# Two layers of graph, attention and expert work on one core: routed experts placed inside the shared expert, and the first attention's keys-values product made narrower

## The reference, cut to what matters

```
# L0_mix, for each of 12 heads of 64, M = 256 random features
phi_q = relu(einsum('bhnd,md->bhnm', q, random_features)); phi_k = relu(...k...)
kv = einsum('bhnm,bhnd->bhmd', phi_k, v)
attn = einsum('bhnm,bhmd->bhnd', phi_q, kv) / M
# L1_ffn, xf = tokens x 768, 8 routed experts of hidden size 1536, top 2 of them for each token
g_s = silu(einsum('td,edf->etf', xf, Wg_s)); u_s = einsum('td,edf->etf', xf, Wu_s)
shared_out = einsum('etf,efd->td', g_s * u_s, Wd_s)
top_vals, top_idx = top_k(xf @ W_router + expert_bias, 2); rw = softmax(top_vals)
routed_out = sum over a token's two experts of rw * ((silu(xf @ Wg_r) * (xf @ Wu_r)) @ Wd_r)
x = x + shared_out + routed_out
```

## Time and profile before

| | |
|---|---|
| median of 3 runs | 2142.15 us (2137.17 to 2149.9) |
| profiled execution, its own time | 2149.02 us |
| its span, first to last instruction | 2147.3 us |
| mean granted PE clock | 0.961 of full |
| PE busy in the span | 2003.2 us, 93% |
| DVE, ACT, POOL busy | 1311.4, 964.7, 89.9 us |

### The profile page before, as it was taken

One profiled execution on the slowest core, in us unless ns is written; L12 is line 12 of the kernel. 1 busy time (PEld: TensorE's weight loads), 2 busy tenths in 40 slices (PEclk: granted clock), 3 DMA queues, 4 the chain that ended last, 5 costly groups with the idle time before them and its releaser, 6 DMA issues. The chain is left out here.

```text
span 2147.3 us, 33807 instructions
## 1 busy us (share of the span) xinstructions
PE 2003.2 (93%) x13496; PEld 1890.5 (88%) x13496; DVE 1311.4 (61%) x1884; ACT 964.7 (45%) x1191; POOL 89.9 (4%) x70
## 2 busy tenths in 40 slices
PE   5899889999999999998999798999889999999996
PEld 4899779999999999997899698899878888888885
DVE  8455477444344345446466547552288988988986
ACT  6344422222111122124566433412167777777775
POOL 0000000000000000000010000000001001001001
PEclk9999789999999999998999889899989999999998
DMA  3311026111112031102200050332199999999997
GB/s 84 104 30 30 21 72 164 61 53 52 52 52 69 31 89 50 44 26 68 59 16 30 7 171 23 125 104 89 46 383 382 387 375 362 380 374 361 380 375 261
DMA packets 186546, 313.62 MB, mean 146 GB/s; under 512 B 13036, under 2 KB 87276, under 8 KB 186018
## 3 DMA queue, kind: packets, MB, share of 16 engines
q1 hardware_dynamic: 181346, 295.31, 39.3%
q0 software_dynamic: 4816, 16.62, 3.4%
q10 hardware_dynamic: 272, 0.07, 0.0%
HBM read 293.48 MB, written 20.40 MB: 146 GB/s over the span
## 5 line engine op out<-in xcount | busy, mean ns | idle before, releaser
L183 PE MATMUL psum<-re_whi,xt_sb 128*128 128x512 f32 (+1 forms) x1680 | 506.8, 376 | 1.6 <-DVE xt_sb L3189 1.6
L183 PE MATMUL psum<-ring_hi,xt_sb 128*128 128x256 f32 (+3 forms) x1920 | 359.1, 285 | 11.9 <-DVE m_v L617 3.9
L183 PEld LDWEIGHTS psum<-re_whi,xt_sb 128*128 128x128 f32 x1680 | 312.5, 188 | 47.0 <-issue 2.0
L3173 DVE TENSOR_TENSOR re_wlo<-moe_raw,re_whi 128x1536 fp32r<-128x1536 f32 x173 | 303.5, 1756 | 35.2 <-ACT re_whi L3127 34.1
L183 PEld LDWEIGHTS psum<-ring_hi,xt_sb 128*128 128x128 f32 (+1 forms) x1920 | 303.6, 190 | 13.2 <-issue 5.3
L183 PE MATMUL psum<-re_wlo,xt_sb 128*128 128x512 f32 (+1 forms) x840 | 312.8, 372 | 0.0
L3127 ACT ACTIVATE re_whi<-moe_raw 128x1536 fp32r<-128x1536 f32 x174 | 258.6, 1489 | 90.8 <-PE psum L183 89.1
L183 PE MATMUL psum<-ring_lo,xt_sb 128*128 128x256 f32 (+3 forms) x960 | 272.7, 284 | 0.0
L183 PEld LDWEIGHTS psum<-ring_lo,xt_sb 128*128 128x128 f32 (+1 forms) x960 | 182.8, 190 | 0.0
L183 PEld LDWEIGHTS psum<-re_wlo,xt_sb 128*128 128x128 f32 x840 | 158.5, 189 | 21.8
L3173 DVE TENSOR_TENSOR re_wlo<-re_more,re_whi 128x1536 fp32r<-128x1536 f32 x84 | 147.6, 1757 | 29.4 <-ACT re_whi L3127 29.4
(11 more groups left out here) (430 smaller groups left out, 3245.1 us busy)
## 6 DMA issues: line engine op xcount, KB each, us to landing
moe_raw<-in_L_ffn_Wg_r SPq DMA_DIRECT2D x74, 768.0 KB, 8.8
moe_raw<-in_L_ffn_Wu_r SPq DMA_DIRECT2D x58, 768.0 KB, 8.5
moe_raw<-in_L_ffn_Wd_r SPq DMA_DIRECT2D x42, 768.0 KB, 6.1
re_more<-in_L_ffn_Wd_r SPq DMA_DIRECT2D x42, 768.0 KB, 9.3
re_more<-in_L_ffn_Wu_r SPq DMA_DIRECT2D x30, 768.0 KB, 7.9
ring_raw<-in_L_gnn_w_rel SPq DMA_DIRECT2D x18, 896.0 KB, 5.1
re_more<-in_L_ffn_Wg_r SPq DMA_DIRECT2D x15, 768.0 KB, 7.2
ring_raw<-in_L_mix_W_qkv SPq DMA_DIRECT2D x24, 384.0 KB, 4.3
```

The costliest lines, as they stand in the source:

```text
L183: mm = pe.matmul(out, lhs[a], rhs[b], start=(first and i == 0), stop=(last and i == 2))
L3173: dve.tensor_tensor(wlo[:, i % RING, :], raw[i % RAWS], whi[:, i % RING, :].bitcast(F32), ALU.subtract)\
```

## The change

1. In the first attention (not the second) `kv` becomes one plane: a head's 64 columns hold the high part, and the other head's 64 columns, zero before, the low part. `attend` issues 16 matmuls in two groups, head 1 into `k.pair[1]`, head 0 into `k.pair[0]`. The two halves of each output are added: ACT copies one half into `at_f` (64 partitions, L612 of after), DVE adds the other. This replaces one ACT copy of 128 partitions.
2. The splits of the next pair's queries move from the end of a pair into the next pair's key tiles 1 and 2, and the split of the second head's keys behind query tile 0. `qk_hi` counts heads now, in both attentions, so `qk_low` starts after the first head's ACT copy.
3. The shared expert's second half moves behind the routed experts, into a block of its own (`phase_shared_last`). The routed block stands after the first half.
4. Job 0's rows are gathered, turned and split inside the first half's `down`, and so is its weight chunk 0 (`preset_low`). The loops start from counts given by small instructions (`credit`).
5. The last job is written out behind the loop and leaves out the work for a next job. In its place SP loads chunks 0 to 2 of the shared expert's second half, and ACT and DVE split chunk 0.
6. The last scatter stands at the start of `phase_shared_last`. `x` is then loaded back from `acc_dram`, the 10 output tiles are added to it, and six transfers store it, each after its tile.

```
             def attend(p):
-                groups = [(num_pair(hd), (2 * hd, 2 * hd + 1)) for hd in (1, 0)] if second else [(k.pair[0], range(4))]
...
+                for hd in (1, 0):
+                    for m in (2 * hd, 2 * hd + 1):
...
+                        for b in range(2):
+                            for h in range(2):
+                                mm = pe.matmul(num_pair(hd)[:, h, 0:HN], kv[:, 0, m, :], phiq[:, m, b, h * HN:(h + 1) * HN],
+                                               start=(m == 2 * hd and b == 0), stop=(m == 2 * hd + 1 and b == 1))
...
         def _(act):
+                    if not second and p >= 1 and t in (1, 2):
+                        qk_high(p, QUERIES, (t - 1,))
...
-                    act.wait_ge(s["at_mm"], p + 1)
-                    act.activation(halves(at_f[:, p, :]), k.pair[0][:, :, 0:HN], ACT.Copy).then_inc(s["at_out"], 1)
+                    for n, hd in enumerate((1, 0)):
+                        act.wait_ge(s["at_mm"], 2 * p + n + 1)
+                        act.activation(halves(at_f[own(hd), p, :]), num_pair(hd)[other(hd), :, 0:HN], ACT.Copy)\
+                            .then_inc(s["at_out"], 1)
...
         def _(dve):
+                for n, hd in enumerate((1, 0) if not second else ()):
+                    at_part = halves(at_f[own(hd), p, :])
+                    dve.wait_ge(s["at_out"], 2 * p + n + 1)
+                    dve.tensor_tensor(at_part, num_pair(hd)[own(hd), :, 0:HN], at_part, ALU.add).then_inc(s["num_f"], 1)
...
+            down(0)
+            turn_first()
+            down(1)
...
-            pe.wait_ge(s["gathered"], 16)
-            turn_gathered(0)
-            turn_gathered(1)
-            count = count_of(pe)
-            with pe.Fori(0, count) as j:
+            pe.sem_inc(s["x_mm"], 2)
+            last = last_of(pe)
+            with pe.Fori(0, last) as j:
+                job(j, False)
+            job(last, True)
...
-            sp.wait_ge(s["all_added"], 1)
-            for r in range(RAWS):
-                sp.wait_ge(loaded[r], count * (16 * NC // RAWS) + (SHARED_LOADS[r] + 16))
-                take_wait(sp)
-            sp.dma_start(out, k.acc_dram[0:NODES, :]).then_inc(s["stored"], 16)
+            src = shared_sources(*shared, 1)
+            for i, r in enumerate((1, 2, 4)):
+                wait_low(sp, last, RAWS + r)
+                take_wait(sp)
+                dst = k.moe_raw[:, i * WE_MOE:(i + 1) * WE_MOE].rearrange("p (k c) -> p k c", c=GC)
+                sp.dma_start(dst, src[i]).then_inc(k.last_loaded[i], 16)
...
+def phase_shared_last(k, name, wg, wu, wd, out):
...
+            load(RAW)
+            sp.wait_ge(s["last_added"], 16)
+            for t, r0, r1 in ROWS:
+                sp.dma_start(k.x[r0:r1, t, :], k.acc_dram[t * P + r0:t * P + r1, :]).then_inc(s["acc_in"], 16)
+            for i in range(RAW + 1, CH):
+                load(i)
+            for t, r0, r1 in ROWS:
+                sp.wait_ge(s["o_read"], TT + t + 1)
+                sp.dma_start(out[t * P + r0:t * P + r1, :], k.x[r0:r1, t, :]).then_inc(s["stored"], 16)
```

More of the change, by code:

```diff
@@ L317, in num_pair @@
         def num_pair(hd):
[L318 removed]
+            return k.pair[0] if hd == 0 else k.pair[3 if second else 1]
         @block.sync
@@ L568, in _ @@
                     act.activation(halves(phiq[:, m, 0, :]), src, FUNC).then_inc(s["pq_hi"], 1)
+                    if m == 0 and p + 1 < PAIRS and not second:
+                        qk_high(p + 1, KEYS, (1,))
                     if m == 0 and p + 1 < PAIRS and second:
@@ L579, in _ @@
                 act.wait_ge(s["kv_f"], p + 1)
-                act.activation(kv[:, 0, :, :], kvf[:], ACT.Copy).then_inc(s["kv_hi"], 1)
-                if p + 1 < PAIRS:
+                if second:
+                    ins = act.activation(kv[:, 0, :, :], kvf[:], ACT.Copy)
+                else:
+                    for hd in range(2):
+                        ms = slice(2 * hd, 2 * hd + 2)
+                        ins = act.activation(kv[:, 0, ms, own(hd)], kvf[:, ms, own(hd)], ACT.Copy)
+                ins.then_inc(s["kv_hi"], 1)
+                if p + 1 < PAIRS and second:
                     qk_high(p + 1, QUERIES)
@@ L696, in _ @@
                     ins.then_inc(s["pq_lo"], 1)
+                    if m == 0 and p + 1 < PAIRS and not second:
+                        qk_low(p + 1, KEYS, (1,))
                 if p >= 1 and p + 5 <= len(st.chunks):
@@ L2957 @@
+            for i in range(2 * TT):
+                c, t = divmod(i, TT)
+                x = k.x[0:TS[t], t, c * GC:(c + 1) * GC]
+                out_ready(dve, i)
+                dve.tensor_tensor(x, out_bank(i)[0:TS[t], 0:GC], x, ALU.add).then_inc(s["o_read"], 1)
+                if i in (TT, TT + 1):
+                    gathered_low(i - TT)
+                if i == TT + 2:
+                    preset_low()
 CH_COLS = 512
@@ L2994, in load_preset, with phase_routed_experts @@
     sp.dma_start(dst, src).then_inc(k.moe_loaded[LOADED_BY[i]], 16)
-def phase_routed_experts(k, name, routed, out):
+def phase_routed_experts(k, name, routed, shared):
     with ExitStack() as ctx:
@@ L3142, in gathered_high, with job @@
                                ACT.Copy).then_inc(s["x_hi"], 1)
-            act.activation(credit[:, 3:4], k.one[:], ACT.Copy).then_inc(s["silu"], HCH)
-            for i in range(HIGH_LEAD):
-                weight_high(0, i)
-            gathered_high(0, 0)
-            gathered_high(0, 1)
-            count = count_of(act)
-            with act.Fori(0, count) as j:
+            def job(j, is_last):
                 for i in range(NC):
@@ L3221, in _ @@
                         dve.tensor_copy(w_now[:], k.job_w[:, bass.ds(j, 1)]).then_inc(s["now_made"], 1)
-                    low(*next_chunk(j, i + LOW_LEAD))
+                    if i + LOW_LEAD < NC or not is_last:
+                        low(*next_chunk(j, i + LOW_LEAD))
+                if is_last:
+                    dve.wait_ge(s["next_hi"], 1)
+                    dve.tensor_tensor(next_lo, k.moe_raw[:, 0:WE_MOE], next_hi.bitcast(F32), ALU.subtract)
+            for n, (name_, by) in enumerate((("lo_done", RAWS + 1), ("used", RING), ("hf", HCH), ("x_lo", 2), ("from_made", 1))):
+                dve.memset(credit[:, 4 + n:5 + n], 0.0).then_inc(s[name_], by)
+            dve.memset(y, 0.0).then_inc(s["y_act"], 2)
+            dve.tensor_copy(to_now[:], k.job_to[:, JOBS:JC]).then_inc(s["now_made"], 1)
+            for i in range(1, LOW_LEAD):
+                low(0, i)
+            last = last_of(dve)
+            with dve.Fori(0, last) as j:
+                job(j, False)
+            job(last, True)
         @block.tensor
@@ L3306, in experts_block @@
         phase_router_shared(k, "rs", *shared, routed)
-        phase_routed_experts(k, "re", routed, out)
-SEM_SETS = (range(100, 160), range(160, 220))
-LASTING_SEMS = range(220, 232)
+        phase_routed_experts(k, "re", routed, shared)
+        phase_shared_last(k, "sl", *shared, out)
+SEM_SETS = (range(100, 158), range(158, 216))
+LASTING_SEMS = range(216, 232)
 class Kit:
```

558 lines of the change are left out of this document (351 added, 207 removed).

## The result

The changed kernel takes 2117.07 us (median of 4 runs, 2113.18 to 2122.08), the kernel before 2144.23 beside it (4 runs, 2137.17 to 2149.9). The ratio is 0.9874, 95% interval 0.9854 to 0.9895: 27 us faster, 3.4 less than the forecast of 30.6, and inside the range. The profiled execution of after has a span of 2111.4 us and is the fastest of its four; that of before was the slowest of its four.

The account below looks back on a forecast made before the run. PE was taken to bound the routed loop (40.17 us a job) and the first attention, with 31 us at the routed stage's ends not PE work. Terms sum to −30.6 us: 2142.15 becomes 2111.6, range 2100 to 2127.

Parts of the forecast that it names:

- what would show it wrong: PE waiting in jobs 0 to 2 for DVE's splits behind a late load, jobs over 40.2 us, or second shared half over 96.
- The start of the routed stage: Between shared half and job 0: PE's pause costs 2.4 instead of 13.8 us; with turning matmuls added, together −10.7 us.
- Chunk 0 is split already. Chunk 1 is not: Job 0's start: chunk 1 ready at 1555.5 at the earliest, PE done with chunk 0 at 1555.0; 0.5 us added.
- transfers too late: Rival, routed stage's start: PE starts job 0 12 us earlier, transfers don't; 3 to 6 us come back, 2117; chance 10%.
- a margin of 5 us: Job 0: chunk 9 lands near 1567, while PE wants it, less 3.4 us for splitting, near 1572.
- PE's clock behind the seam: Routed stage after its opening pause: 1.7 of the 2.7 us lost at lower clock remain, a gain of 1.0 us.
- Last job and new seam: Routed stage's end: last job drops six turning matmuls, −0.7 us; pause of 1.0 us before second shared half, +1.3 with slack.
- Tail: After PE's last matmul: 5.7 us, bounds 5.2 to 9.8, instead of 17.4, so −11.7 us.
- First attention: Eight fewer matmuls per pair −8.0, waits +1.7, shorter pause −1.0, DVE addition at the end +0.9: −6.4 us, bounds −9 to 0.
- The second rival, additions on the path: Rival, first attention: DVE not free in time in each pair, waits of 1 us and more take the saving; 2118; chance 15%.
- Second attention: DVE starts a split after ACT's first head, 0.7 us earlier, removing PE's waits in 5 pairs: −1.4 us, at worst 0.
- The slower rival: Routed loop: transfers set the pace; at 353 GB/s a job takes 42.3 us, at 345 the kernel takes 2155; chance 3%.

Follow-up runs that it names:

- with the read moved: Changed kernel with three-chunk splitting, early loads and stores, three loads issued ahead, plus PE reading the last job's number inside the shared block: 2105.55 us, 0.9808 of the kernel before.
- splits alone: Changed kernel, but ACT and DVE split chunks 0, 1 and 2 of job 0 inside the shared block, not only 0: 2116.68 us, 0.9865 of the kernel before.
- transfers alone: Changed kernel, but chunks 6 and 7 of job 0 and four stores of x are issued inside the shared block: 2111.99 us, 0.9837 of the kernel before.
- both with the loads ahead: Changed kernel with three-chunk splitting, early loads and stores, and loads of chunks 9 to 11 inside the shared block: 2104.68 us, 0.9809 of the kernel before.
- more stores: Changed kernel with another 1.9 MB of stores of x, to an unused tensor, before the first loop loads: 2128.3 us (one run).

## Why the prediction was right, point by point

The time came out as forecast because what it missed was of both signs, and that is luck. Between the two traces the routed stage is 10.0 us worse than forecast; the first attention is 8.5 better, the tail 2.0, the second attention 1.9, and 2.6 are not of the change. The prediction also named what would show it wrong: that PE waits in jobs 0 to 2 for DVE's splits behind a late load. PE did, in job 0. By its own sign the account of the routed stage's start was wrong.

**The start of the routed stage: size right, one consequence missed.** The pause is 2.16 us for 2.4. The read of the job number and the entry of the loop were given 1.0 us; with the read moved the pause is 1.52, so the read is worth 0.6 to 1.0 us at least, as DVE ends the pause there. The step that failed is the next one, "Chunk 0 is split already. Chunk 1 is not", with 0.5 us for it. It looked at the first wait only. The old 13.8 us of PE's pause were also the time in which ACT and DVE got their ring ahead: ACT had made six splits and DVE five when PE began. Now DVE owes eight, 13.4 us, before the first hidden product, which PE wants after 10.8.

**The rival "transfers too late" was the case, at 10%, and too cheap.** It was dismissed by a margin of 5 us: chunk 9 some 14 us behind PE's start at 384 GB/s, and wanted 19 us behind it. The margin was worked out wrong twice. Nine chunks of 2.1 us are the 19 us already, so with 3.4 for splitting off, the margin was some 2 us. And the chunk that PE waits through is not 9 but 12, whose split stands ahead of the second hidden product in DVE's program; PE wants that product after 81 matmuls, also some 19 us in. Chunk 9 came 17.5 us behind PE's start (1437.16 to 1454.67), 18.1 behind SP's first issue. Its issue stands at 1446.97, 4.5 us behind the end of the last store's issue, a step that was not counted. Its price was put at 3 to 6 us; the two pauses are 9.5 us and the clock behind them costs some 4, read from the same groups of products at full clock, so that the routed stage is 10 us over its forecast of 563.4 although the later jobs gave 2.1.

**PE's clock behind the seam** was taken as 1.7 us lost. With the pauses gone the stage takes 561.4 us, where 14 jobs of 40.01 less the 0.7 of the last one's turning are 559.4: 2.0 us lost, of which 1.6 are in the 45 products (12.11 for 10.49). The size was right where the clock fell, and it does not always fall: the 45 products took 12.11 to 12.14 us in five traces after pauses of 2.15 to 2.49 us, 10.83 and 10.49 in two after 2.16 and 2.17, and 10.49 in one after 1.52.

**Last job and new seam: right.** 0.93 us of pause for 1.0, and the clock stayed at full, as forecast (1.00 from 2010 to 2014 us). The half takes 96.3 us for 96.0, with a wait of 1.13 us for a split of DVE inside it that was there before too (1.15).

**Tail: right in kind, mis-sized.** 3.7 us for 5.7. The two issues take 0.67 together, not 0.6 each, and the landing with what follows it 2.4 for 3.9.

**First attention: the largest wrong size, −6.4 for some −10 to −15.** Eight matmuls less are 1.2 us a pair, as said. The pause before query tile 2 was thought to shrink by 0.2 and went altogether; and where it showed 0.51 us its going gave 0.67 (moved splits alone: 24.10 to 23.43). The wait on the addition is 0.25, within the 0.2 to 0.4. In the last pair the clock gave 4 us more, in most of the traces. The second rival, additions on the path, has the wait of 0.79 us in the kernel without the moved splits, but not its price: even that kernel kept 7.7 us by its ratio.

**Second attention: −3.3 for −1.4.** Five waits of 0.3 us were counted. The ten traces with heads counted one by one have 152.3 to 153.0 us for 156.2. Two pairs are 28.2 us apart there for 28.7, and the last pair gives 1.2 us, which is not explained.

**The slower rival fell.** Transfers ran at 384 GB/s in job 1 as before and at 372 near the end, and jobs did not grow longer. The 384 GB/s speak against the limit of about 358 GB/s of the Trainium skill, page "DMA: Bandwidth & Descriptors", section "Specifications", here too.

## What to carry to other kernels

When a pause is removed, list every engine that worked during it, not only the one that waited: each has lost that head start, and the next wait of the bound engine shows which. An engine that works in the order of its program passes on a late input to results that do not need it; so look for the last step that stands ahead of the wanted one. Two causes in a row hide each other, and mending the first alone moves nothing (routed time: splits alone −1 us, transfers alone −8, both with the loads ahead −12). Loads that fill a ring for a loop belong ahead of the reads and the branch that open it.

## What the runs showed of the hardware that was not expected

SP needed 4.1 to 4.7 us between its last store issue ahead of the loop and its first load inside it, with one job number and two expert numbers to read, in five traces. With the same reads it was 2.8 us in the kernel before, 3.5 with more stores, and 2.5 with three loads ahead, so part of it is something else, which stays open. PE's one read cost 0.6 to 1.0 us. A pause of PE that its row gives as 0.51 us cost 0.67. The granted clock behind pauses of 2.15 to 2.19 us, and in the last attention pair, differs from one execution of like code to the next, by 1.3 to 1.7 us and 4 us.
